# Two tiles of every edge group fetched row by row from the sync engine instead of by gathers

## What is computed

```python
# first layer: sum the edges' own features by source node
agg = jnp.zeros_like(x).at[row].add(edge_attr)            # row = src, 100000 x 256
...
h = jnp.concatenate([x, agg, x_with_cond], axis=1)
h = jax.nn.relu(h @ W1.T + b1)
return h @ W2.T + b2
...
# second layer: sum a table of the nodes, picked by src, by destination node
msg = jax.nn.sigmoid(w * ht[src] + b_param)
fsum = jax.ops.segment_sum(msg, dst, num_segments=num_nodes)
```

## Time and profile before

| | |
|---|---|
| median of 3 runs | 2470.68 us (2470.21 to 2475.73) |
| the profiled execution, timed | 2474.17 us |
| its span in the profile | 2471.2 us |
| mean granted PE clock | 0.912 of full speed |
| busy share: PE, DVE, POOL, ACT | 82%, 76%, 66%, 57% |
| gathers on POOL | 785 in each stage |

### The profile page before, as it was taken

One profiled execution on the slowest core, in us unless ns is written; L12 is line 12 of the kernel. 1 busy time (PEld: TensorE's weight loads), 2 busy tenths in 40 slices (PEclk: granted clock), 3 DMA queues, 4 the chain that ended last, 5 costly groups with the idle time before them and its releaser, 6 DMA issues.

```text
span 2471.2 us, 35853 instructions
## 1 busy us (share of the span) xinstructions
PE 2033.5 (82%) x8987; PEld 1413.0 (57%) x8987; DVE 1890.1 (76%) x4857; ACT 1412.2 (57%) x4944; POOL 1622.3 (66%) x1656
## 2 busy tenths in 40 slices
PE   5778898889889888878987677987887887798885
PEld 3345565566556556645876445655554554575564
DVE  7867778978978986896776787788698789763377
ACT  5554476557548547655348443754664574485476
POOL 0077777777777777773027777777777777777703
PEclk6588899999989989999998998998998899899898
DMA  5033334343443333341437333333343333344438
GB/s 156 4 113 112 118 114 122 117 121 113 118 120 113 119 116 113 111 120 58 160 131 262 105 118 103 114 118 101 113 122 99 111 113 111 106 135 148 139 89 152
DMA packets 143876, 292.18 MB, mean 118 GB/s; under 512 B 31227, under 2 KB 73963, under 8 KB 143659
## 3 DMA queue, kind: packets, MB, share of 16 engines
q0 software_dynamic: 80800, 211.13, 30.4%
q1 hardware_dynamic: 61211, 76.68, 9.5%
q10 hardware_dynamic: 1668, 2.11, 0.3%
HBM read 250.46 MB, written 39.33 MB: 117 GB/s over the span
## 4 chain that ended last, share of the span: by engine, by line
PE 42%; DVE 27%; issue 12%; POOL 7%; DMA 7%; ACT 3%; DVEq 2%; SPq 1%; ACTq 0%; POOLq 0%
PE bank L1393 40%; DVE agg L1193 13%; POOL store L631 7%; DVE hits L1122 3%; DMA store<-g_table,idx_all 3%; DVE oh L1126 2%; DMA store<-in_edge_attr,idx_all 2%; DVE store L1126 2%; DVEq L1185 1%; DVE hit L1118 1%; DVE oh L1118 1%; DMA w1bT<-turned_scratch 1%; ACT oh L822 1%; DVE cum L1079 1%; ACT dist L814 1%
## 5 line engine op out<-in xcount | busy, mean ns | idle before, releaser
L1393 PE MATMUL bank<-store,oh 128*128 (+1 forms) x4900 | 1319.6, 403 | 306.4 <-DVE agg L1193 106.0
L1393 PEld LDWEIGHTS bank<-store,oh 128*128 128x128 f32 (+1 forms) x4900 | 831.5, 186 | 670.2 <-issue 364.1
L1193 DVE TENSOR_TENSOR agg<-bank,agg 128x256 f32 x2050 | 860.2, 420 | 383.2 <-PE bank L1393 283.6
L631 POOL DMA_INDIRECT store<-in_edge_attr,idx_all x785 | 777.9, 991 | 357.8 <-issue 151.5
L631 POOL DMA_INDIRECT store<-g_table,idx_all x785 | 766.9, 977 | 242.7 <-issue 149.7
L822 ACT ACTIVATE oh<-dist 128x128 f32<-128x128 f32 x2050 | 527.5, 301 | 459.6 <-PE bank L1393 436.0
L814 ACT ACTIVATE dist<-iota,nloc_all 128x128 f32<-128x128 f32 x2050 | 648.2, 387 | 90.3 <-DVE nloc_all L1167 87.1
L1393 PE MATMUL bank<-oh,hit 125*128 125x314 f16 x800 | 170.5, 341 | 26.4 <-DVE oh L1126 25.9
L1122 DVE TENSOR_TENSOR hits<-iota,ttab 125x628 f16<-125x628 f16 x400 | 191.1, 478 | 0.0
L1126 DVE TENSOR_TENSOR oh<-hits,v 125x628 f16<-125x628 f16 x400 | 184.8, 481 | 3.6
L1126 DVE TENSOR_TENSOR store<-hits,v 125x628 f16<-125x628 f16 x400 | 184.4, 481 | 4.0
(11 more groups left out here) (207 smaller groups left out, 1891.9 us busy)
## 6 DMA issues: line engine op xcount, KB each, us to landing
store<-in_edge_attr,idx_all POOLq DMA_INDIRECT x785
store<-g_table,idx_all POOLq DMA_INDIRECT x785
store<-in_x SPq DMA_DIRECT2D x48, 256.0 KB, 4.0
pre_scratch<-late SPq DMA_DIRECT2D x25, 256.0 KB
store<-pre_scratch SPq DMA_DIRECT2D x25, 256.0 KB, 2.6
turned_scratch<-oh SPq DMA_DIRECT2D x25, 256.0 KB, 3.4
g_table<-store SPq DMA_DIRECT2D x25, 256.0 KB, 3.5
w1bT<-turned_scratch SPq DMA_DIRECT2D x25, 256.0 KB, 3.1
```

Source lines behind the costliest of these rows:

```text
L631: gp.indirect_dma_start(out=store[:, at % RING * D:(at % RING + 1) * D], out_offset=None, in_=table_dram, in_offset=bass.IndirectOffsetOnA ...
L1193: dve.tensor_tensor(to, job_bank(n)[0][:, 0:D], to, ALU.add).wait_op(s_mm, n + 1, "sem-ge").then_inc(s_acc, 1)
L1393: return pe.matmul(o, l, r, start=start, stop=stop, skip_group_check=skip)
```

## The change

Tiles 118 and 156 of each group (counted from 0; the 119th and the last, short one) are no longer gathered. Each has a slot of its own behind the ring (slots 70 and 71 of `store`). SP copies the row numbers of both tiles out of their columns of `idx_all` into one partition (`row_numbers`, `edge_rows`), reads them into registers 16 at a time, and issues one DMA of 1 KB for each row (`fetch`), 128 rows for tile 118 and 32 for tile 156. In SP's program the rows of tile 118 stand at steps 11 to 112 and those of tile 156 at steps 113 to 150. The first row of a tile waits until the slot's last reader in the group before is done. PE waits at job 118 and job 156 for all rows of the tile (`s_fetch`).

A job's slot is no longer its tile's number modulo 64. The slots stand in a small table, `slotc`, which POOL and DVE make once at the start; PE picks from it by two matmuls in `job_biases`, and DVE copies the result to `slot_all` (one operation in place of three).

```diff
+FETCHED = (118,) + (TILES - 1,)
+FIRST_SLOT = 70
+LAST_ROWS = EG - P * (TILES - 1)
+ROW_LOADS = 16
...
         def rows_landed(beat):
-            return 16 * sum(TB if b % BEATS < BEATS - 1 else TILES - TB * (BEATS - 1) for b in range(beat % SLOTS, beat + 1, SLOTS))
+            return 16 * sum(gathered(b % BEATS) for b in range(beat % SLOTS, beat + 1, SLOTS))
+
+        def gathered(beat):
+            return sum(t not in FETCHED for t in range(beat * TB, min(beat * TB + TB, TILES)))
+
+        def fetches(g):
+            rows = {}
+            begin = 0
+            for i, t in enumerate(FETCHED):
+                begin, stop = max(begin, t + TAILS - TILES + 2), t - 6
+                for r in range(0, fetched_rows[i]):
+                    rows.setdefault(begin + (stop - begin) * r // fetched_rows[i], []).append((i, r))
+                begin = stop + 1
+            return rows
...
+            def row_numbers(g):
+                sp.wait_ge(s_dec, g + 1)
+                for i, t in enumerate(FETCHED):
+                    sp.dma_start(edge_rows[:, i * P:i * P + fetched_rows[i]],
+                                 idx_all[0:fetched_rows[i], table(g, t, TILES)]).then_inc(s_rownum, 16)
+
+            def fetch(table_dram, g, i, r):
+                if r == 0:
+                    if i == 0:
+                        sp.wait_ge(s_rownum, 16 * len(FETCHED) * (g + 1))
+                    if g:
+                        sp.wait_ge(s_mm, NTH[g - 1, FETCHED[i] + TAILS] + 1)
+                    elif i == len(FETCHED) - 1:
+                        sp.wait_ge(s_slotc, SLOTC)
+                if r % ROW_LOADS == 0:
+                    stop = min(r + ROW_LOADS, fetched_rows[i])
+                    _, values = nc.values_load_multi_w_load_instructions(
+                        edge_rows[:, i * P + r:i * P + stop], [mybir.EngineType.SP], min_val=0, max_val=table_dram.shape[0] - 1,
+                        skip_runtime_bounds_check_because="an edge's or a node's number")
+                    numbers.update((r + j, v) for j, v in enumerate(values))
+                sp.dma_start(store[r:r + 1, fetched_at[i]], table_dram[bass.ds(numbers.pop(r), 1), :]).then_inc(s_fetch[i], 16)
...
             for g in STAGES[0]:
+                rows = fetches(g)
                 for t in range(TILES):
+                    for i, r in rows.get(t, ()):
+                        fetch(a["edge_attr"], g, i, r)
...
             def gathers(table_dram, g):
                 gp.wait_ge(s_dec, g + 1)
                 stage = 0 if g < G1 else 1
                 for t in range(TILES):
+                    if t in FETCHED:
+                        continue
...
-                job_windows(False).then_inc(s_nl, 1)
+                job_windows(False)
+                if sig == 0:
+                    pe.wait_ge(s_slotc, SLOTC)
+                for k, rows in ((0, P), (1, TREST)):
+                    r = mm(pS[0:64, 0:JT], slotc[0:rows, k, sig:sig + 1].to_broadcast([rows, 64]), pick[0:rows, k, :], k == 0, k == 1)
+                r.then_inc(s_nl, 1)
...
                         if p < TILES and p % TB == 0:
                             beat = beat_of(g, p)
                             pe.wait_ge(s_g[beat % SLOTS], rows_landed(beat))
+                        if p in FETCHED:
+                            i = FETCHED.index(p)
+                            pe.wait_ge(s_fetch[i], 16 * fetched_rows[i] * (g_ + 1))
                         sum_job(g_, p)
```

More of the change, by code:

```diff
@@ L143, in gnn_program @@
         agg = sb("agg", [P, NW * CH])
-        store = sb("store", [P, (NW + 2 * CHB) * CH])
+        store = sb("store", [P, FIRST_SLOT * D + len(FETCHED) * D])
         oh = sb("oh", [P, CHB * CH])
@@ L157, in gnn_program @@
         nloc_all = sb("nloc_all", [P, 2 * JT])
-        off_all = sb("off_all", [1, 2 * JW], I32)
-        slot_all = sb("slot_all", [1, 2 * JW], I32)
-        lagr = sb("lagr", [1, JT], I32)
+        tables = sb("tables", [P, 2 * JW], I32)
+        slot_i = sb("slot_i", [P, 2 * SORTS], I32)
+        slotc = sb("slotc", [P, 2, SORTS])
         code = sb("code", [P, TILES], F16)
@@ L213, in gnn_program @@
         sums_at = (pA, pB, pS, pR)
+        off_all, slot_all, edge_rows = tables[0:1, :], tables[32:33, :], tables[96:97, 0:P * len(FETCHED)]
+        fetched_at = [slice((FIRST_SLOT + i) * D, (FIRST_SLOT + i + 1) * D) for i in range(len(FETCHED))]
+        fetched_rows = [P if t < TILES - 1 else LAST_ROWS for t in FETCHED]
         def slot2k(t, n):
             return t[:, n * CH:(n + 1) * CH]
-        pre, ring = store[:, 0:NW * CH], store[:, NW * CH:]
+        pre, ring = store[:, 0:NW * CH], store[:, NW * CH:FIRST_SLOT * D]
         ohv = oh[:, 0:OHS * SW].rearrange("p (k n) -> p k n", n=SW)
@@ L305, in gnn_program @@
         s_rank, s_off = sem("s_rank"), sem("s_offsets")
+        s_slots, s_slotc, s_rownum = sem("s_ringslots"), sem("s_slotcolumns"), sem("s_rownumbers")
+        s_fetch = [sem(f"s_fetched{i}") for i in range(len(FETCHED))]
         s_ps = sem("s_prestore")
@@ L335, in gnn_program @@
         CONSTS = 10
+        SLOTC = 2 + len(FETCHED)
         MASKS = 1 + KD * (P // DH)
@@ L508, in _ @@
                         column_starts(g + 1)
+                row_numbers(g + 1)
             sp.wait_ge(s_ps, 16 * NW)
@@ L562, in _ @@
             upper_load(0)
+            for q in range(CHB):
+                sp.wait_ge(s_gs[q], 16 * CBODIES)
             for g in STAGES[1]:
+                rows = fetches(g)
                 for t in range(TILES):
+                    for i, r in rows.get(t, ()):
+                        fetch(g_dram[:, :], g, i, r)
                     if (g, t) in UPPER_STORES:
@@ L570, in _ @@
                         column_starts(g + 1)
+                if g + 1 < SORTS:
+                    row_numbers(g + 1)
             for at, n in UPPER_STORES.items():
@@ L610, in _ @@
                              pattern=[[0, P]], channel_multiplier=-1).then_inc(s_gi, 1)
+            gp.iota(slot_i[:, :], pattern=[[P, 2], [TILES, SORTS]], base=0, channel_multiplier=1).then_inc(s_slots, 1)
             gp.memset(epsilon[:, :], EPS).then_inc(s_tail, 1)
             gp.memset(slot2k(x_all, NW - 1), 0.0).then_inc(s_tail, 1)
+            gp.memset(store[:, fetched_at[-1]], 0.0).then_inc(s_slotc, 1)
+            gp.wait_ge(s_slots, 2)
+            gp.tensor_copy(slotc[:, :, :], slot_i[:, :].rearrange("p (k g) -> p k g", k=2)).then_inc(s_slotc, 1)
+            for i, t in enumerate(FETCHED):
+                at = slotc[:, t // P, :]
+                gp.wait_ge(s_slotc, 2 + i)
+                gp.affine_select(out=at, in_=at, compare_op=ALU.not_equal, fill=float((FIRST_SLOT + i) * D), base=-(t % P),
+                                 pattern=[[0, SORTS]], channel_multiplier=1).then_inc(s_slotc, 1)
             gp.wait_ge(s_std, 1)
@@ L1629, in sum_job @@
                     _, values = nc.values_load_multi_w_load_instructions(
-                        slot_all[0:1, load_of(g, p)], [mybir.EngineType.PE], min_val=0, max_val=(RING - 1) * D,
-                        skip_runtime_bounds_check_because="a number below 64 times 256")
+                        slot_all[0:1, load_of(g, p)], [mybir.EngineType.PE], min_val=0, max_val=(FIRST_SLOT + len(FETCHED) - 1) * D,
+                        skip_runtime_bounds_check_because="a number of a ring slot times 256")
                     slots.update(((g, p + i), v) for i, v in enumerate(values))
```

15 lines of the change are left out of this document (6 added, 9 removed).

## The result

| | before | after |
|---|---|---|
| median of 5 runs | 2470.21 us (2464.22 to 2475.73) | 2453.24 us (2452.76 to 2455.3) |
| profiled execution, its span | 2474.17, 2471.2 us | 2452.99, 2451.2 us |
| mean granted PE clock | 0.912 | 0.917 |

The ratio is 0.9937 (0.9924 to 0.995): 15.6 us of 2470 less (12 to 19), where 21.7 were forecast (2470.68 to 2449). The time lies in the range, 4 us above the number.

A forecast was written before the change was run, and what follows sets the result against it. POOL's unbroken gathers were taken as the bound; 11.7 - 1.3 + 11.5 = 21.9 us saved, additions at nothing, so 2474.17 - 21.9 = 2452.3 us profiled, or 2449 us against the 2470.68 us median. Range 2443 to 2460 us.

The forecast's parts named there:

- The bound: Both stages: POOL gathers without a break, one each 1.299 us in stage 0 and 1.282 us in stage 1; others wait.
- What the change removes: Nine counting gathers a stage, 11.7 us and 11.5 us, less 1.3 us for the ring: 21.9 us.
- the tenth gather of a stage: Tile 156 of groups 4 and 9, with no gather behind it in its stage: removing it counts for nothing.
- The 1.3 us for the ring in group 4: Stage 0, group 4: the ring's limit on POOL's lead takes back 1.3 us of the gain, bounds 0 and 2.6.
- What it adds: Row issues on SP, two PE matmuls a group, small DVE and POOL operations: all hidden, costed at nothing.
- The cost of a row: On SP, issue, register operation and share of the register read: 0.39 us a row, 62 us a group of 200.
- The limit of 1.2 us a row: On SP: the 160 rows fit into a group as long as one costs under about 1.2 us.
- PE's cover: Late in a group, 3.7 us of PE's 6.1 us idle gets used; landing waits shorten by some 2 to 4 us.
- That the jobs become the bound: Rival, 10%: in stage 0 POOL's lead is lost and PE's matmuls show, 4 to 6 us less gain, 2454 to 2459.
- That SP is held up and the gain is given back: Rival, 7%: rows hold SP at `column_starts` or `upper_load`, PE starts late, 2 us each in most groups; 2463 to 2478.
- That SP becomes the bound: Rival, 10%: rows over 1.2 us make PE wait at jobs 118 and 156; 2610 us at 1.3 us, some 3850 at 2.1.
- The number: Whole kernel: 2452.3 us against the profiled execution, 2449 us against the median of the runs; own forecast 73%.

The follow-up runs named there:

- the kernel with the gathers kept: The change, but POOL also gathers tiles 118 and 156 into ring slots that no job reads; 2472.84 us, ratio 1.0017 to the kernel before.
- the repeat of the change: The changed kernel with only an empty line added, run and profiled a second time; 2450.42 us, ratio 0.9929 to the kernel before.
- the third tile: The change with tiles 75, 140 and 156 fetched by rows instead of 118 and 156; ratio to before 0.9879 (2441.88 us), on a slow chip 1.0815.
- own slots: The change without row fetches: POOL gathers tiles 118 and 156 into slots 70 and 71, slot table kept; ratio to before 1.0011, on a slow chip 1.0018.

## Why the prediction was right, and where its size was off

**The bound.** Right. POOL's gathers set the time: taking ten a stage away gives 20 us, each of the two tiles has its part (12.4 and 8.2 us, each about 4 either way), and five more a stage give 13.6 us more (about 5 either way). The stretch between the stages, without gathers, did not move (206.9 and 207.2 us).

**What the change removes.** 21.9 us forecast, 19.8 us by the kernel with the gathers kept (21.7 by the repeat of the change), all within the uncertainty. That the tenth gather of a stage is worth nothing fits the unchanged stretches behind tile 155's gather, 206.9 to 207.2 us and 123.5 to 123.3 us (repeat); it was not tried by itself. The 1.3 us for the ring in group 4 are the weak term. The prediction read one longer wait there; the trace before has five gaps over 0.3 us, from 1015 to 1033 us, of which 1.3 us is the longest, together 2.4 us over the usual 0.30. In the first profile of the change they are gone, which gives 2.4 us back instead of taking 1.3, and 11.7 + 2.4 is the 14.1 us that stage 0 gained. In the repeat there are seven, 3.9 us over the usual, 1.5 us more than before, and stage 0 gained 11.8 us. So the term has no fixed value, and its bounds, 0 to 2.6, leave out what the first profile had. The last gather of stage 0 came at 1122.1 us, not near 1127: 1.0 us of that is an earlier start, the rest the stretch itself, 14.1 us shorter and not 10.4.

**What it adds.** "All of this I cost at nothing" is the term that was mis-sized. The additions cost 0.17%, 4 us of the time (2 to 6); the slot table alone measured 2.7 us (0 to 5), so it may be the larger part, which the intervals do not decide. The prediction looked for a new wait, on PE, on SP or on DVE, and found none, rightly: there is none in the trace. What grew is the stretch from a stage's first gather to its last, by 1.9 and 1.5 us with the gathers kept and by 2.6 and 4.3 us with the table alone. The bound is an engine that hardly waits, so its time grows when its own instructions get longer. In stage 1 they did in each kernel with the table on the ordinary chips, 979 to 983 ns in the mean against 977. In stage 0 they did where tile 156 is still gathered, 994 to 996 ns against 991; the change itself has 991 and its repeat 989. Each of these is one profile, and the two profiles of the change differ by 2 and 1 ns, so longer gathers are the likely place of the cost and not a shown one. The last line of the prediction named them ("gathers that take longer beside SP's issues") without a price, and the neighbour is not needed: the mean is also higher where SP issues no rows. What in the table would draw them out, the two matmuls, the one DVE operation that took the place of three, or only the moved order of DVE's work, was not tried and stays open.

**The cost of a row.** 0.39 us forecast. From one row to the next it is 0.41 us, which agrees, but the read of registers was taken as 0.59 us for 16 when the earlier trace rows show it for 8: 16 take 1.23 us, 0.077 us a row. With it a row is 0.48 us, 77 us a group and not 62. It changed nothing, since SP has 200 us. The limit of 1.2 us a row fits the group as a whole, (202 - 8) / 160 = 1.21; in the steps of tile 118, with 1.27 rows each, 1.25 us a step leaves 0.98. At 0.48 neither was tried.

The Trainium skill, page "DMA: Bandwidth & Descriptors", section "Anatomy of one DMA", gives a DMA issued from GpSimd a fixed cost of about 2.0 us, and puts most of it down to the confirmation of landing, not to the issue. The rows are issued from SP, and here, as the prediction had it, no such cost is their pitch: rows leave 0.41 us apart, and doubling those of tile 118 changed the ratio from 0.9937 to 0.9935. How long a single row takes to land no run here shows.

**PE's cover.** PE's two matmuls and the rows' semaphores made no wait that the trace shows, and PE waits less for landings, but 1.3 us a group less and not "2 to 4"; in single windows it went both ways.

**The rivals.** That the jobs become the bound: no, POOL waits for nothing over 0.4 us with 775 gathers (1.0 us in the repeat) and over 0.3 us with 770. (Its 4 to 6 us on top of 2449 would be 2453 to 2455 us, not 2454 to 2459, so the time alone could not have told it from the forecast; POOL's waits do.) That SP is held up and the gain is given back: no; PE waits 7.9 us for `w1bT` in all, where it was 14.3 before. That SP becomes the bound: not on the ordinary chip, at 0.48 us a row. (At 2.1 us a row the prediction's own sum gives 2470 + 1420 = 3890 us, not 3850.) But the mechanism of the third was right, and that of the second with it: on a chip where a row takes 0.7 to 0.9 us, 288 rows no longer fit into a group, SP's loads behind them are late, and the time rises by 8%. The threshold of 1.2 us, for 160 rows, was not tried. Whether the change itself, with 160 rows a group, is faster or slower than before on such a chip was not run. An estimate from its parts there: rows +0.9 to +1.1%, table +0.2%, 18 gathers of 1.0 to 1.2 us -0.6 to -0.8%, together 0.3 to 0.7% slower, which is about what the two such chips differ by.

**The number.** Against the profiled execution the forecast is nearly exact, 2474.17 - 21.9 = 2452.3 and 2452.99 measured, but partly by luck. Stage 0 gained 14.1 us where 10.4 were forecast, stage 1 9.1 for 11.5 (in the repeat 11.8 and 8.2); 1.0 us came at the start and 1.2 us around the span; against them stand 3.8 us at the end, with the lower clock of this one execution, and 0.3 us between the stages. The 4 us that the additions cost are inside the stages' figures. Against the medians, whose start was 3.5 us lower, the miss is 4 us, the size of the cost that was put at nothing.

## What to carry to other kernels

When the bound is an engine that issues gathers without a pause, count its instructions: each one moved to an engine with idle issue time is worth its full pace, here 1.3 us, for as long as the receiving engine's rows fit into the same group; work out that limit, and use the room up to it (the third tile brought some 13.6 us more). Ask of an addition not only who will wait for it but whether it makes the bounding engine's instructions longer, and test it alone, with the gain taken out. A longest wait says nothing on how many there are: sum them. A design that leans on thousands of small instructions can be the better one on one chip and the worse on the next, so look at the longest instruction and not at the median, and measure the kernel before on the same chip each time.

## What the runs showed of the hardware that was not expected

- Two of the chips ran the same kernel in 2794 and 2813 us, where it took 2467 to 2475 elsewhere. The medians of SP's row instructions and of the gathers are the same. What differs: SP's row instructions are drawn out to 1.4 us (a register operation of 37 ns in the median took 1.408 us at most), idle time put down to "issue" grows (PE 160.5 us against 7.5 with own slots), and the mean granted clock is 0.87 against 0.91.
- A read of registers from SBUF took the longer the more registers it filled: 1.23 us for 16 on SP, 0.59 us for 8 on PE.
- After the same wait of 2.5 us PE was granted 0.74 of its clock over the next stretch in one execution and 0.97 in another of the same instructions, and the end of the program took 4 us longer with the first.
- 1600 single-row DMAs, or 2880, beside 770 to 775 gathers a stage left the gathers' median at 946 to 947 ns.
